# Experts over all tokens, or over tokens sorted by expert into tiles of 128

## The reference

```python
logits = (einsum('bsh,eh->bse', nf, gate_weight) + gate_bias).astype(bfloat16).astype(float32)
scores, idx = top_k(logits, 2)
combine = sum(one_hot(idx, 8) * softmax(scores)[..., None], axis=-2)
p1 = einsum('bsh,eoh->bseo', nf, mlp1_weight) + mlp1_bias      # 8 experts x 512 outputs
g, lin = minimum(p1[..., 0::2], 7), clip(p1[..., 1::2], -7, 7)
act = g * sigmoid(1.702 * g) * (lin + 1)
p2 = einsum('bsei,ehi->bseh', act, mlp2_weight) + mlp2_bias
combined = einsum('bseh,bse->bsh', p2, combine)
```

## Time and profile before

| | |
|---|---|
| runs | 1202.9, 1203.91, 1199.92 us; median 1202.9 |
| profiled execution | 1205.98 us, of which the span of the core is 1204.1 |
| mean granted TensorE clock | 0.906 |
| busy, share of the span | PE 81%, DVE 69%, ACT 58%, POOL 35% |
| data moved by DMA | 110.08 MB |

### The profile page before, as it was taken

How to read it: one execution, slowest core, us unless ns; L and a number is a source line. 1 busy time by engine, 2 the same in 40 slices (tenths; PEclk the granted TensorE clock), 3 DMA queues, 4 the chain that set the end, 5 groups by cost and what they waited for, 6 DMA issues and landing times.

```text
span 1204.1 us, 18696 instructions
## 1 busy us (share of the span) xinstructions
PE 974.9 (81%) x5241; PEld 414.1 (34%) x5313; DVE 828.1 (69%) x1622; ACT 697.5 (58%) x905; POOL 424.8 (35%) x360
## 2 busy tenths in 40 slices
PE   4608897889679897987778997888799999996564
PEld 1302222233233443333233343323343344344243
DVE  5732102669658797677676799586867897797797
ACT  2318895856448574765448665675567676771232
POOL 2413303433244333533235333542232333233243
PEclk9858998989889999988799898999989899997587
DMA  4254454324424252434413345352534353421011
GB/s 150 74 108 79 102 104 99 88 74 97 116 59 130 77 117 82 102 96 95 119 37 103 98 108 118 71 128 67 114 86 107 97 125 82 101 76 58 31 53 31
DMA packets 80001, 110.08 MB, mean 91 GB/s; under 512 B 22523, under 2 KB 56707, under 8 KB 76803
## 3 DMA queue, kind: packets, MB, share of 16 engines
q1 hardware_dynamic: 61444, 83.47, 29.9%
q10 hardware_dynamic: 18432, 25.17, 7.0%
HBM read 82.89 MB, written 25.69 MB: 90 GB/s over the span
## 4 chain that ended last, share of the span: by engine, by line
PE 49%; DVE 25%; issue 13%; ACT 4%; DMA 3%; POOL 2%; SPq 2%; another core or an unknown queue 1%; DVEq 0%; ACTq 0%; POOLq 0%
PE OP L687 13%; PE S L673 12%; PE D L659 8%; DVE th_sb L1103 3%; DVE act_sb L1108 3%; PE A L642 3%; PE D L569 3%; PE D L586 3%; PE BB L642 3%; DVE acc L1098 2%; DVE g_sb L1086 2%; DVE l_sb L1088 2%; DMA X<-in_x 2%; DVE xn L946 2%; ACT probs L804 2%
## 5 line engine op out<-in xcount | busy, mean ns | idle before, releaser
L804 ACT ACTIVATE probs<-S 128x1024 f32<-128x1024 f32 x512 | 511.8, 1022 | 256.2 <-PE S L673 253.4
L673 PE MATMUL S<-Qs,Ks 98*128 98x512 bf16 x1024 | 312.4, 399 | 61.8 <-issue 23.0
L687 PE MATMUL OP<-probs,V 128*17 128x512 f32 x2048 | 280.1, 620 | 2.7 <-ACT O L813 2.7
L891 POOL TENSOR_TENSOR act_lo<-act_sb,act_hi 128x512 fp32r<-128x512 f32 x128 | 165.5, 1293 | 212.3 <-DVE act_hi L1114 152.4
L673 PEld LDWEIGHTS S<-Qs,Ks 98*128 98x128 bf16 x1024 | 81.4, 101 | 249.0 <-ACT probs L804 98.7
L659 PE MATMUL D<-W,act_hi 128*128 128x256 f32 x448 | 135.6, 333 | 29.5 <-DVE Vn L986 16.2
L1098 DVE SCALAR_TENSOR_TENSOR acc<-D,combh,acc 128x256 f32<-128x256 f32 x224 | 97.1, 475 | 82.5 <-PE D L659 82.1
L1103 DVE SCALAR_TENSOR_TENSOR th_sb<-th_sb,g_sb 128x512 f32<-128x512 f32 x128 | 129.6, 1012 | 0.7 <-ACT th_sb L780 0.7
L885 POOL TENSOR_SCALAR W<-W2b 128x512 fp32r<-128x512 bf16 x64 | 45.4, 709 | 217.4 <-PE D L659 212.1
L1108 DVE SCALAR_TENSOR_TENSOR act_sb<-l_sb,th_sb 128x512 f32<-128x512 f32 x128 | 107.2, 837 | 16.7 <-POOL act_lo L891 12.2
L659 PE MATMUL D<-W,act_lo 128*128 128x256 f32 x448 | 116.3, 290 | 0.0
(11 more groups left out here) (136 smaller groups left out, 1016.7 us busy)
## 6 DMA issues: line engine op xcount, KB each, us to landing
W<-in_w ACTq DMA_DIRECT2D x64, 256.0 KB, 2.7
Ks<-k_scr SPq DMA_DIRECT2D x32, 384.0 KB
W2b<-in_w ACTq DMA_DIRECT2D x64, 128.0 KB, 2.7
Ks<-k_scr SPq DMA_DIRECT2D x32, 256.0 KB
o_scr<-O SPq DMA_DIRECT2D x32, 256.0 KB, 4.5
q_scr<-parts SPq DMA_DIRECT2D x16, 384.0 KB, 3.1
k_scr<-parts SPq DMA_DIRECT2D x16, 384.0 KB, 2.6
Qs<-q_scr SPq DMA_DIRECT2D x32, 192.0 KB
```

The lines of the kernel that those rows point to most:

```text
L673: last = mm(S[:, j2, C * i:C * (i + 1)], Ks[0:SROWS + MROWS, g % 2, j, P * kt:P * (kt + 1)], Qs[0:SROWS + MROWS, g % 2, j, :], start=True, ...
L687: last = mm(OP[32 * j:32 * j + VW, :], V[:, kt, HG * g + j, :], probs[:, s % 2, C * j:C * (j + 1)], start=kt == 0, stop=kt == KT - 1)
L804: nc.scalar.activation(probs[:, s % 2, 2 * C * j2:2 * C * (j2 + 1)], S[:, j2, :], ACT.Exp, scale=SCALE).then_inc(exp_done, 1)
L891: tt(act_lo[:, e % 2, it, :], act_sb[:, a % 2, :], act_hi[:, e % 2, it, :].bitcast(FP32), ALU.subtract).then_inc(lo_s, 1)
```

## The change

The experts no longer run over all 512 tokens of a unit. Each token's two choices (1024 rows in all) are given places in a list of 15 **tiles** of 128 rows, in which every tile belongs to one expert. For this PE counts choices per expert with triangular and all-one matrices (`rank`), and DVE turns the counts into places `pos` and an expert number per tile, `eid` (`place_slots`). POOL writes the normalized rows to memory by 8 indirect DMAs (`scatter`). Two tiles make a **pair**, and a unit has 8 pairs (the last has one tile). For a pair SP reads the expert numbers into registers and loads the two weight sets of each tile (`wl`), loads its rows (`xg`), PE turns them (`gx`) and applies the first matrices as 12 matmuls of 128 columns per tile, of which 4 add the bias, then the second as 4 of 256 columns; DVE copies the result to `ysb`, and SP stores it. After the last pair POOL reads every token's two rows back by 8 indirect DMAs (`gather`), and DVE adds them to `acc` with their gates (`combine`). The second matrices are turned to fp32r once and kept in memory. EXPERTS now begins at half 40 with six halves a pair, and ends at half 97.

```diff
 NCH = L // C
 TC = C // P
-NF = 2 * NE
+NT = C * TOPK // P + NE - 1
+NPAIR = (NT + 1) // 2
+SLOTS = NT * P
+BLOCKS = 2 * FI // P
...
-          18, "ms": 18, "rrms": 20, "nf": 22, "nfT": 24, "logits": 26, "gates1": 26, "etop": 27, "gates2": 28,
-          "combT": 32, "b20": 33, "b21": 34}
-    FFN0, LAG, PAIRED = 26, 4, True
-    DOWN, TANH, HIDDEN, UP, LO, W2AT = 0, 2, 2, 1, 5, 3
+          18, "ms": 18, "rrms": 20, "nf": 22, "nfT": 24, "logits": 26, "gates1": 26, "etop": 27, "rank": 30, "gates2": 30, "scatter": 33,
+          "combT": 34}
+    FFN0, PACE = 40, 6
+    WL, XG, TANH, HIDDEN, LO, DOWN, STORE = -4, -3, 3, 4, 5, 8, 9
+    UP = 2
...
     for st in ("x1_in", "x1_b", "stats2", "rstd2", "xc", "ss", "ms", "rrms", "nf", "nfT", "logits", "gates1", "etop",
-               "gates2", "combT"):
+               "rank", "gates2", "scatter", "combT"):
...
-    ORDER = ("down", "tanh", "hidden", "w2", "lo", "up", "final")
...
+    for m in range(NPAIR):
+        h = FFN0 + PACE * m
+        for st, off in (("wl", WL), ("xg", XG), ("gx", 0), ("up", UP), ("tanh", TANH), ("hidden", HIDDEN), ("lo", LO),
+                        ("down", DOWN), ("store", STORE)):
+            place(EXPERTS, h + off, (st, m))
+    h = FFN0 + PACE * (NPAIR - 1) + DOWN
+    for a in range(2):
+        place(EXPERTS, h - 4 + 2 * a, ("b2", a))
+    place(EXPERTS, h + 2, ("gather", 0))
+    place(EXPERTS, h + 6, ("combine", 0))
+    place(EXPERTS, h + 7, ("final", 0))
+    FINAL = (h + 7) // 2
+
+    ORDER = ("gx", "up", "down", "tanh", "hidden", "lo", "store", "wl", "xg", "b2", "gather", "combine", "final")
...
-        act_lo = sb("act_lo", [P, 2, CT, C], FP32R)
+        W1 = sb("W1", [P, 4, CT, BLOCKS * P], BF16)
+        W2 = sb("W2", [P, 4, CT * E], FP32R)
+        xg = sb("xg", [P, 2, 2, E], BF16)
+        xgT = sb("xgT", [P, 2, 2 * CT * P], BF16)
+        act_hi = sb("act_hi", [P, 2, C], FP32R)
+        act_lo = sb("act_lo", [P, 2, C], FP32R)
+        ysb = sb("ysb", [P, 2, C], FP32)
+        yg = sb("yg", [P, TC, TOPK, E], FP32)
         g_sb = sb("g_sb", [P, 2, C], FP32)
...
-                return (A[:, :], s_banks[0])[i % 2], (BB[:, :], s_banks[1])[i % 2], s_banks[2 + i % 2]
-            return A[:, :], BB[:, :], D[:, :]
+                return ((U[:, :, :], S[:, 0, :].rearrange("p (q t) -> p q t", q=2))[m % 2],
+                        S[:, 1, C * (m % 2):C * (m % 2 + 1)])
+            return U[:, :, :], D[:, :]
+
+        def tiles_of(m):
+
+            return min(2, NT - 2 * m)
...
+                elif st == "wl":
+                    wait_apart(sp, (gating, GATING * u + TILED))
+                    if not looped(u) and u == 0 and a == 0:
+                        wait_apart(sp, (w2_w, 32))
+                    if looped(u) or u or a >= 2:
+                        wait_apart(sp, (m2_mm, NPAIR * u + a - 1))
+                    for q in range(tiles_of(a)):
+                        t, to = 2 * a + q, 2 * (a % 2) + q
+                        e = sp.value_load(eid[0:1, t:t + 1], min_val=0, max_val=NE - 1)
+                        sp.dma_start(W1[:, to, :, :], w1[bass.ds(e, 1)].rearrange("o p c n -> (o p) c n")).then_inc(w_ld[a % 2], 16)
+                        sp.dma_start(W2[:, to, :].bitcast(FP32), w2f[bass.ds(e, 1)].rearrange("o p n -> (o p) n")).then_inc(w_ld[a % 2], 16)
+                elif st == "xg":
+                    sp.wait_ge(sc_s, 16 * TOPK * TC * (u + 1))
+                    if looped(u) or u or a >= 2:
+                        sp.wait_ge(xgT_s, NPAIR * u + a - 1)
+                    nt = tiles_of(a)
+                    sp.dma_start(xg[:, a % 2, 0:nt, :], xs[n][2 * P * a:2 * P * a + P * nt, :].rearrange("(q p) c -> p q c", p=P)
+                                 ).then_inc(xg_ld[a % 2], 16)
+                elif st == "store":
+                    sp.wait_ge(y_s, NPAIR * u + a + 1)
+                    nt = tiles_of(a)
+                    sp.dma_start(ys[n][2 * P * a:2 * P * a + P * nt, :].rearrange("(q p) c -> p q c", p=P),
+                                 ysb[:, a % 2, 0:E * nt].rearrange("p (q c) -> p q c", c=E)).then_inc(y_w[a % 2], 16)
...
+                    mm(bank[:, 0:width], tri[:, :], each, start=True, stop=False)
+                    for d in range(1, TC):
+                        mm(bank[:, NE * d:width], ones[:, :], each[:, 0:width - NE * d], start=False, stop=d == TC - 1)
+                    for t in range(TC):
+                        last = mm(bank[:, width:width + NE], ones[:, :], each[:, NE * t:NE * (t + 1)], start=t == 0, stop=t == TC - 1)
+                    last.then_inc(d_full, 1)
...
+                elif st == "gx":
+                    pe.wait_ge(xg_ld[a % 2], rows_in(u, a))
+                    for q in range(tiles_of(a)):
+                        for c in range(CT):
+                            i = CT * q + c
+                            last = nc.tensor.transpose(bank[:, :].bitcast(BF16)[:, P * i:P * (i + 1)], xg[:, a % 2, q, P * c:P * (c + 1)],
+                                                       identb[:, :])
+                    last.then_inc(d_full, 1)
...
-                gate, linear, _ = expert_banks(u, f)
-                for gl, bank in ((0, gate), (1, linear)):
-                    if gl and alone(u) and f >= 2:
-                        pe.wait_ge(l_s, NF * u + f - 1)
-                    elif gl and not alone(u) and f:
-                        pe.wait_ge(l_s, NF * u + f)
-                    for c in range(CT):
-                        last = mm(bank, W1[:, e % 2, c, FI * gl + P * it:FI * gl + P * (it + 1)], nfT[:, c, :],
-                                  start=c == 0, stop=c == CT - 1)
-                    last.then_inc(m1_mm, 1)
...
+            def expert_up(m, u):
+
+                i = NPAIR * u + m
+                pe.wait_ge(xgT_s, i + 1)
+                pe.wait_ge(w_ld[m % 2], weights_in(u, m))
...
+                bank, _ = pair_banks(u, m)
+                for q in range(tiles_of(m)):
+                    for k in range(BLOCKS):
+                        cols = slice(P * k, P * (k + 1))
+                        mm(bank[:, q, cols], b1_sb[:, cols], oneh[:, 2 * m + q:2 * m + q + 1].to_broadcast([NE + 1, P]), start=True, stop=False)
+                        for c in range(CT):
+                            r = P * (CT * q + c)
+                            last = mm(bank[:, q, cols], W1[:, 2 * (m % 2) + q, c, cols], xgT[:, m % 2, r:r + P],
+                                      start=False, stop=c == CT - 1)
+                last.then_inc(m1_mm, 1)
...
+                i = NPAIR * u + m
+                pe.wait_ge(lo_s, i + 1)
...
+                _, bank = pair_banks(u, m)
+                for q in range(tiles_of(m)):
                     for k in range(4):
                         it, part = k // 2, (act_hi, act_lo)[k % 2]
-                        last = mm(bank[:, E * q:E * (q + 1)], part[:, e % 2, it, tok:tok + P], W2[:, e % 2, E * it:E * (it + 1)],
+                        r = FI * q + P * it
+                        last = mm(bank[:, E * q:E * (q + 1)], part[:, m % 2, r:r + P], W2[:, 2 * (m % 2) + q, E * it:E * (it + 1)],
...
-                        wait_apart(act, (m1_mm, 4 * NE * u + 4 * (e + 1)), (w2_s, NE * u + e + 1))
-                        load_expert((e + 2) % NE)
...
-                elif st == "w2":
...
-                        nc.gpsimd.tensor_scalar(W2[:, e % 2, :], W2b[:, e % 2, :], 1.0, 1.0, ALU.mult, ALU.mult).then_inc(w2_s, 1)
...
+                elif st == "scatter":
+                    wait_apart(pool, (gating, GATING * u + PLACED), (nf_s, TC * (u + 1)))
...
+                    for k in range(TOPK):
+                        for t in range(TC):
+                            i = TC * k + t
+                            nc.gpsimd.indirect_dma_start(xs[n], bass.IndirectOffsetOnAxis(ap=pos[:, n, i:i + 1], axis=0),
+                                                         nf[:, t, :], None).then_inc(sc_s, 16)
+                elif st == "gather":
+                    wait_apart(pool, *((y_w[i], rows_in(u, NPAIR - 1)) for i in range(2)))
+                    for t in range(TC):
+                        for k in range(TOPK):
+                            i = TC * k + t
...
+                            nc.gpsimd.indirect_dma_start(yg[:, t, k, :], None, ys[n],
+                                                         bass.IndirectOffsetOnAxis(ap=pos[:, n, i:i + 1], axis=0)).then_inc(yg_ld[t], 16)
...
+                    if looped(u) or u:
+                        dve.wait_ge(sc_s, 16 * TOPK * TC * u)
...
+                elif st == "rank":
+                    dve.wait_ge(d_full, k + 1)
+                    place_slots(u, n, bank)
...
+                elif st == "gx":
+                    w = P * CT * tiles_of(a)
+                    dve.wait_ge(d_full, k + 1)
+                    if looped(u) or u or a >= 2:
+                        dve.wait_ge(m1_mm, NPAIR * u + a - 1)
```

(27 more changed lines are left out.)

285 lines of the change are left out of this document (154 added, 131 removed).

## The result

The changed kernel takes 1656.5 us (median of four runs, 1650.3 to 1670.1) against 1202.9 us before: a ratio of 1.379, 95% interval 1.370 to 1.388. The prediction was 1186 us, range 1130 to 1248. It is wrong in sign and far outside its range. The profiled execution took 1658.4 us, with a span of 1656.5.

What follows compares the result with a forecast made beforehand. It took attention to be bound by PE's work plus PE's waits for VectorE. 1206.0 - 99 (removed work) + 25 (GpSimd) + 10 (weights) + 47 (tail) = 1189, against the runs' median 1186 us; range 1130 to 1248.

Steps and rivals of the forecast that it cites:

- The failed step: Weight loads in attention: 6.0 us to landing, covered by 11.7 us between `wl` and `up`, except right behind a stack.
- 10 in attention: Cost of weight loads in attention that come right behind a stack on SP's queue: 10 us in all.
- +18 and +17: Tail: +18 us before `up` of the last unit, +17 us for its experts, at 9.9 us a pair.
- rival (d): Weights come late in attention as well, behind a stack: 51 us, of which 10 are counted, 1227 us; chance 0.12.
- Rival (c): Weight loads of PE's small matmuls don't overlap: 0.102 us each, not 0.056, 63 us more, 1249 us; chance 0.08.
- 0.8 us for an indirect DMA: Time one indirect DMA holds GpSimd, 16 a unit, bounded at 0.43 and 1.28 us.
- rival (a): GpSimd's queue becomes the bound, at 1.28 us an indirect DMA: 1232 us; chance 0.26.
- my term of 25 us: GpSimd's indirect DMAs in attention: 5 us in each of four middle units, 5 us in units 1, 6 and 7.
- The prediction's -99: Work removed from the experts in attention: 63 us on PE and 36 us on VectorE.
- 71 over 6.8 units: PE's work in attention, 198 us before and 127 after: 71 us less, the upper bound of PE's saving.
- +47: Tail: the sum of +18 before the last unit's `up`, +17 for its experts and +12 at its end.
- A tail well over 175 us: Sign that the forecast is wrong; a right forecast would show a tail of 160 to 170 us.

Runs made afterwards that it cites:

- e1: Changed kernel with the load of a pair's rows three halves earlier, ahead of the weights in SyncE's queue: 1516.6 us.
- e16: e10 with the experts' weights loaded once only, so results are of wrong experts: 1286.5 us.
- e2: Changed kernel with each weight load from the second unit on bringing only 16 columns, same issues and waits: 1611.2 us.
- e15: e10 with each weight load from the second unit on bringing only 16 columns, same issues and waits: 1376.3 us.
- e9: e1 with the experts' weights loaded once only and the bias matmuls left out: 1271.9 us.
- e10: e1 with the bias matmuls reading 128 rows in place of 9, filled up with zeros, same result: 1421.0 us.
- e6: e1 with the 16 indirect DMAs of a unit replaced by plain ones to fixed rows on SyncE's queue: 1524.9 us.
- e8: e9 with the 16 indirect DMAs of a unit replaced by plain ones issued by SyncE: 1249.2 us.
- e4: Changed kernel with the experts' weights loaded for the first two pairs and never again: 1436.0 us.
- e3: Changed kernel with the bias matmuls left out, and with them the bias from the result: 1502.3 us.
- e14: e10 with the weights' register loads, issues and waits on ScalarE's queue in place of SyncE's: 1456.0 us.
- e17: e10 with the stage `wl` placed one half later: 1455.4 us.
- e18: e10 with the stages `down` and `store` placed one half earlier: 1412.0 us.

## Why the prediction was wrong, step by step

**The failed step: the weights.** It read "In attention six halves, 11.7 us, lie between `wl` and `up`, so it is covered, except right behind a stack". It asked only when `up` needs the weights. It never asked what else stands behind `wl` in SyncE's queue, though I had the order in hand: `wl` waits for `down` of m-2, then come its issues, then `xg`, and the consumer of `xg` is `gx`, four halves after that `down`, not six. Four halves of 1.96 us are 7.8; the loop above takes 10.6 from start to start. The rows had no term in the sum. By e1 that was 140 us; by e16 the rest of the reload another 135, where I had 10 in attention and, in the tail, parts of +18 and +17. Only 45 us of the reload go with the bytes (e2 and e15). The chance of 0.12 for late weights, rival (d), put them at `up` and priced them at 41 us.

**Small matmuls: the row was right, the case another.** 0.056 us from the earlier trace rows holds for 16 in a row in e9 and for 24 in e10. The Trainium skill's 81 ns (TensorE: Matmul & The Clock Gate, section Back-to-back issue gap), which I had weighed, is above both, so that the measurement decides. What I missed is that these 24 are no run of like matmuls: every third reads 9 rows. Two changes a block at 0.1 us cost 96 us (e10 against e1). My transposes all read 128 rows, so their row could not tell. Rival (c) had the right sign and a wrong mechanism.

**GpSimd.** I took 0.8 us for an indirect DMA. Its timeline shows

```profile
822.82 0.97 POOL L965 DMA_INDIRECT xs<-nf,pos  x1 [0.30 <-issue]
824.09 0.96 POOL L965 DMA_INDIRECT xs<-nf,pos  x1 [0.30 <-issue]
825.36 0.96 POOL L965 DMA_INDIRECT xs<-nf,pos  x1 [0.30 <-issue]
```

one each 1.27 us, the upper end of my bounds and rival (a)'s price. All 128 of them lasted between 0.94 and 1.31 us, so that no long mutual blocking is seen. GpSimd did not decide: e6 shows no gain from moving them to SyncE, e8 23 us. That this is near my term of 25 us is luck: the term stood for attention alone and for 0.8 us each, while e8 gives 13 us there at 1.27. (Its 3.4, 6.4 and 2 us up to `combine` also add up to 11.8 and not 11.6, which changes nothing.) Rival (a) had 46 for that price.

**The saved work.** VectorE's saving is there, and none of it shows in the time. From the window of 300 to 1000 us in e16, which has neither the reload nor changes of row count, and waits for rows only three times (36 us):

```profile
300.00:1000.00 700.00, 547.25 (x3567) 231.49 (x3582) 352.46 (x804) 385.54 (x487) 249.04 (x213) 0.88 0.41 101
```

Before, the same window had PE 604.1 and DVE 526.1 us (clock 0.93). A unit lasts 148.6 us in e16 and 140.2 before (mean of the four middle ones), so by these shares TensorE went from about 121 to 116 us per unit and VectorE from 105 to 75, while the unit became 8 us longer. TensorE saved half of the 10 us a unit that 71 over 6.8 units make. The prediction's -99 took the share of the chain that the experts' lines had and scaled it down. That step failed too: the four middle units did not become shorter by their removed work. I read it as work that leaves a chain of hand-overs and is replaced by waiting for the next link, which no run isolates. Most of the 8 us lies in the second head group of each unit: 26.2 us before, 33.4 in e16, in the unit at 641 and 652 us. TensorE is busy 24.0 and 25.4 us of it, so its work is the same, and the chain there runs through norm, `th_sb` and `l_sb` of the experts, ScalarE's `parts` and exponentials, and the routing on VectorE. I take it as a longer chain of hand-overs, unproven likewise.

**The tail.** I had +47, measured +115. Of this, e1 takes 26 (208.4 us), e10 another 18 (189.9), e16 another 41 (148.9); 30 are left, for store, gather, scatter and sums without attention beside them. A pair took 15.0 to 16.0 us and not 9.9, because the rows' 3.3 to 4.6 us follow the weights' issues, and `up` took 4.4 us at half clock.

**The whole account.** 1656.5 us less 140 (rows behind weights) less 96 (change of row count) less 135 (reload: 45 bytes, 90 issues, waits and lateness) is 1286.5 but for rounding, and 84 of that lie above the kernel before: 30 in the tail and some 50 in attention. The shares hold in this order, since the costs overlap: taken out first, the reload alone gives 221 (e4) and no bias 154 (e3). The first three are shown by edits, the last is located but its cause is only argued. Even with the three out the kernel is 84 us slower than before, where the forecast, with its own costs counted, had it 17 faster. What part of the 90 is issue time in SyncE's queue and what part the weights' lateness at `up` also stays open: e14 changed both and added ScalarE's own stall, and e17 and e18 changed the order of the queue too.

**The signs.** "A tail well over 175 us" came true. Waits of `up` for weights, the sign of (d), appear only once the rows are out of the way (15 us in e1, 25 in e10). The sign that mattered, TensorE waiting for rows, was not on the list.

## What to carry to other kernels

When a transfer gets a wait in a queue that executes in order, list everything issued behind it and give each its own deadline, from the instruction that ends the wait to the first consumer: here the weights had six halves, and the rows behind them four. After moving a stage, read the new order of the queue before reading the time: e17 and e18 also put a store in front of the weights. Price a matmul from a row with the same neighbours, not only of the same size; a small helper matmul of few rows between large ones can cost more than what it stands between, and here zero rows were cheaper than the change. And work taken out of an engine that is not alone on the path may be worth nothing, as here: test the gain with the new costs taken out, before taking them for the reason.

## What was new of the hardware

- 128-column bf16 matmuls, each with its own load of 128 x 128 weights, follow each other every 0.056 us at full clock, 16 and 24 in a row. A change between 9 and 128 rows costs about 0.1 us each way: 0.37 us for a block of three with two changes, 0.17 with none. From 128 to 98 rows no such cost shows (two matmuls in 0.12 us).
- An indirect DMA of 128 rows holds GpSimd for 0.95 to 0.97 us in the median, plus 0.30 us to the next.
- GpSimd as the issuer of this kernel's stores and row loads is worse than SyncE: 13 and 32 us in 1421 for 64 and 128 transfers, waits included.
- A load of 128 KB that lands in 2.2 us with no weights on the queue (e9, median) took 3.8 in the changed kernel, 4.7 right behind 1 MB of weights in the loop shown and 3.3 to 4.6 in the last unit's.
- In a tail in which TensorE was busy 94 of 234.5 us the granted clock was 0.51, nearly the lower of its two levels (1.2 GHz) throughout; in the tail before, with 70 busy of 119, it was 0.74.
